# Reordering TensorE's slot in a Mamba-2 scan: square sums behind the off-diagonal products, group products ahead of the diagonal ones

## The chip, the cores and the metric

The kernel runs on one core of one Trainium2 chip (trn2). The metric is the device time of one execution in microseconds. Three runs of the kernel before gave 1118.15, 1118.6 and 1119.61 us; their median, 1118.6 us, is the time before.

## What is computed

The reference is two transformer-like blocks with adaptive layer norm. The first one holds the part that is changed: a Mamba-2 layer (32 heads of 128 channels, 8 groups, state size 128) over 2 batches of 512 tokens, model width 256. The rest (two mixture-of-experts layers and an attention layer over sorted keys) is the same in both kernels. Cut to the scan:

```python
hbc = silu(conv4(proj))                      # causal convolution of 4 taps, then hs, B, C
Y_diag = einsum('bclhn,bcshn,bhcls,bcshd->bclhd', Cc, Bc, Lmat, Xc)
states = einsum('bclhn,bhcl,bclhd->bchdn', Bc, decay_states, Xc)
Y_off  = einsum('bclhn,bchdn,bhcl->bclhd', Cc, states_prev, state_decay)
y = (Y_diag + Y_off).reshape(b, s, H, P) + D_res
g = (y * silu(gate)).reshape(b, s, I // gs, gs)      # gs = 512 channels = 4 heads
h = g * rsqrt(mean(g * g) + EPS)
return norm_w * h @ out_proj_w.T
```

The mean of squares runs over the 4 heads of one norm group. The kernel multiplies the unnormalised heads by the output weights and scales the product by the group's root afterwards.

## The kernel before, in words

The scan works on 64 pairs of batch and head (N = 64), in chunks of 128 tokens. It is a software pipeline of slots, s = 0 to 69, written out by hand: every engine has its own `scan_slot(s)`, and only semaphores tie them together. In slot s head s begins (`h0`), head s-1 is in its second slot (`h1`), head s-2 in its third (`h2`), and one tile of 128 tokens of an earlier norm group is projected out (`e`). Every fourth slot, with s mod 4 = 2, begins a new norm group for `e` (`e[0] == 0`). The text below calls a slot by **its kind, s mod 4** (kind 0 to 3); four slots are a period.

**TensorE, in order** (lines 502 to 582):

- px: six bf16 products of 512 columns, the x projection (L513, recorded as L439 with tile wA and wAl);
- kind 2 only, sq: sums over the partitions of the squares (L521), which wait for GpSimd's last addition of squares (`sq_add`);
- t: four transposes of the convolved head (L532), which wait for VectorE's xT (L1401);
- o: off-diagonal products (L540), which wait for the states (L1370);
- w: one tile of the output projection (L552);
- d: diagonal products (L564), which wait for Mm (L1341), Xdt (ScalarE, L938), and VectorE's yv (L1381) of the head before, whose bank they overwrite;
- s: state products (L573), which wait for GpSimd's Xw (L1825);
- group_slot (L576; lines 480 to 500), in slots 0 to 47 only: a part of the products of group 4 + s//4. Kind 0 and 1: g, a projection half of six products (L439 with tile wbs), for B and for C; kind 2: k, four transposes of B (L453); kind 3: m, the C x B products (L459);
- pg: six products, the gate projection.

**VectorE, in order** (lines 1321 to 1414): Mm (L1341), gs (L1345), yv (L1381, waits for o), three taps of the convolution (L1354), three state steps (L1367 for the first, a copy out of PSUM that waits for s; L1370 for the others), xT (L1401), acc (L1412, takes the tile of w). Then its own group_slot: three taps of the group (L1273) in kind 0 and 1, with BT (L1281) ahead of them in kind 1, and CT (L1289) in kind 2. In kind 2 the twelve steps of the root, `root(0)` to `root(11)`, each of 4 elements a partition, are strewn between these: step 0 (L1424) reads sq's sums out of PSUM, the others (L1427, L1432, L1435, L1437, L1440) read and write SBUF alone. BT and CT too read SBUF alone; the taps, Mm, gs, yv, xT and acc read PSUM.

**GpSimd, in order** (lines 1813 to 1861): Xw (L1825, waits for Xdt), yb = yv * gs (L1835, waits for yv), wAl (L1842), CE (L1846), wB scaled (L1852), sqa += ysq (L1858, not where the head is the first of its norm group, which is kind 2), and in kind 3 the mask of CB (L1810), which the trace shows at the start of the next slot. All of them read SBUF. ScalarE evaluates the tanh and exp functions and turns PSUM into SBUF; SyncE loads weights ahead of their use.

Of the kernel before, what the change touches and what calls it, by code (L numbers as in the profile page):

```python
# [8 lines left out]
B, S, D = 2, 512, 256  # L9
T = B * S  # L10
P = 128
KT = D // P
NT = T // P
TB = S // P
# [15 lines left out]
N = B * H  # L30
# [13 lines left out]
def build_block(nc, io, stop=None):  # L44
# [4 lines left out]
    with ctx:  # L49
# [6 lines left out]
        bank = [ctx.enter_context(nc.psum_tensor(f"bank{n}", [P, 512], fp32)) for n in range(8)]  # L56
# [8 lines left out]
        ident, tri, ones = cst[:, 0:P], cst[:, P:2 * P], cst[:, 2 * P:3 * P]  # L65
# [61 lines left out]
        sqa = sb("sqa", [P, 2, S])  # L127
# [107 lines left out]
        q = {n: sem(n) for n in names}  # L235
# [130 lines left out]
        def _(pe):  # L366
# [48 lines left out]
            for t in range(NT):  # L415
                for kt in range(KT):
                    last = nc.tensor.matmul(bank[4][:, t * H:(t + 1) * H], hT[:, kt, t * P:(t + 1) * P],
                                            wdt[:, kt, :], start=kt == 0, stop=kt == KT - 1)
# [11 lines left out]
            for b in range(B):  # L430
                last = nc.tensor.transpose(bank[7][:, b * P:(b + 1) * P], csq[:, b * P:(b + 1) * P], ident)
# [48 lines left out]
            def group_slot(s):  # L480

                gq, r = FIRST + s // 4, s % 4
                if gq >= B * G:
                    return
                if r == 0:
                    pe.wait_ge(q["c_evac"], 2 * gq)
                    if s == 0:
                        pe.wait_ge(q["csr_done"], 1)
                    group_half(gq, 0, bank[7][:, :]).then_inc(q["c_proj"], 1)
                if r == 1:  # L490
                    pe.wait_ge(q["c_step"], 6 * gq + 3)
                    group_half(gq, 1, bank[7][:, :]).then_inc(q["c_proj"], 1)
                if r == 2:
                    pe.wait_ge(q["c_step"], 6 * gq + 6)
                    pe.wait_ge(q["c_bc"], 2 * gq + 1)
                    turn_keys(bank[7])
                if r == 3:
                    pe.wait_ge(q["c_evac"], 2 * gq + 1)
                    pe.wait_ge(q["c_bc"], 2 * gq + 2)
                    meet(gq, bank[7])  # L500

            def scan_slot(s):

                h0, h1, h2, e = head(s), head(s - 1), head(s - 2), out_tile(s)
                if h0:
                    n, b, hid = h0
                    w = (wAh[:, n % 4, :], wAl[:, n % 2, :])
                    pe.wait_ge(q["wsplit"], n + 1)
                    if n == 0:
                        pe.wait_ge(q["c_step"], 6 * (FIRST - 1))  # L510
                    else:
                        pe.wait_ge(q["cv_step"], 3 * n)
                    split_product(bank[0][:, :], lambda a, kt: w[a][:, kt * P:(kt + 1) * P],  # L513
                                  lambda a, kt: hTs[:, a, kt, b * S:(b + 1) * S]).then_inc(q["px"], 1)
                if e and e[0] == 0:
                    k = e[1]
                    if s - 1 < N:
                        pe.wait_ge(q["rc_step"], 3 * (s - 1))
                    pe.wait_ge(q["sq_add"], 3 * (k + 1))
                    for t in range(TB):  # L520
                        last = nc.tensor.matmul(bank[4][:, S - P + t:S - P + t + 1], sqa[:, k % 2, t * P:(t + 1) * P],  # L521
                                                ones[:, 0:1], start=True, stop=True)
                    last.then_inc(q["ssq_done"], 1)
                if h1:
                    n = h1[0]
                    pe.wait_ge(q["xT_done"], n + 1)
                    if n:
                        pe.wait_ge(q["xdt_done"], n)
                    else:
                        pe.wait_ge(q["c_evac"], 2 * FIRST)  # L530
                    for t in range(TB):
                        last = nc.tensor.transpose(bank[2][:, t * P:(t + 1) * P],  # L532
                                                   xT[:, n % 4, t * P:(t + 1) * P], ident)
                    last.then_inc(q["tr_x"], 1)
                if h2:
                    n = h2[0]
                    pe.wait_ge(q["rc_step"], 3 * n + 3)
                    pe.wait_ge(q["ce_done"], n + 1)
                    for c in range(1, TB):
                        last = nc.tensor.matmul(bank[5][:, c * P:(c + 1) * P], St[:, n % 2, (c - 1) * P:c * P],  # L540
                                                CE[:, n % 2, (c - 1) * P:c * P], start=False, stop=True,
                                                skip_group_check=True)
                    last.then_inc(q["py"], 1)
                if e:
                    t, k = e
                    if t == 0:
                        pe.wait_ge(q["wo_done"], HG * (k + 1))
                        pe.wait_ge(q["yb_done"], HG * (k + 1))
                    if TB * k + t:
                        pe.wait_ge(q["oa_done"], TB * k + t)  # L550
                    for m in range(HG):
                        last = nc.tensor.matmul(bank[6][:, 0:D], yb[:, HG * (k % 2) + m, t * P:(t + 1) * P],  # L552
                                                wB[:, k % 2, m, :], start=m == 0, stop=m == HG - 1)
                    last.then_inc(q["out_done"], 1)
                if h1:
                    n = h1[0]
                    pe.wait_ge(q["xdt_done"], n + 1)
                    pe.wait_ge(q["M_done"], n + 1)
                    if n:
                        pe.wait_ge(q["yc_done"], n)  # L560
                    else:
                        pe.wait_ge(q["c_step"], 6 * FIRST)
                    for c in range(TB):
                        nc.tensor.matmul(bank[5][:, c * P:(c + 1) * P], Xdt[:, n % 2, c * P:(c + 1) * P],  # L564
                                         Mm[:, n % 2, c * P:(c + 1) * P], start=c == 0, stop=c == 0,
                                         skip_group_check=True)
                    if n:
                        pe.wait_ge(q["rc_step"], 3 * n)
                    if e and e[0] == 0:
                        pe.wait_ge(q["rg_step"], ROOT * e[1] + 1)  # L570
                    pe.wait_ge(q["xw_done"], n + 1)
                    for c in range(TB - 1):
                        last = nc.tensor.matmul(bank[4][:, c * P:(c + 1) * P], Btok[:, h1[2] % G, c, :],  # L573
                                                Xw[:, n % 2, c * P:(c + 1) * P], start=True, stop=True)
                    last.then_inc(q["ps"], 1)
                group_slot(s)  # L576
                if h0:
                    n, b, hid = h0
                    if n:
                        pe.wait_ge(q["gs_done"], n)  # L580
                    split_product(bank[1][:, :], lambda a, kt: w[a][:, (KT + kt) * P:(KT + kt + 1) * P],
                                  lambda a, kt: hTs[:, a, kt, b * S:(b + 1) * S]).then_inc(q["pg"], 1)
# [574 lines left out]
        def _(dve):  # L1157
# [147 lines left out]
            def group_slot(s):  # L1305

                gq, r = FIRST + s // 4, s % 4
                if gq >= B * G or r == 3:
                    return
                if r == 1:  # L1310
                    keys(gq)
                if r == 2:
                    queries(gq)
                    return
                dve.wait_ge(q["c_raw"], 2 * gq + r + 1)
                for d in (1, 2, 3):
                    if d > 1:
                        dve.wait_ge(q["c_step"], 6 * gq + 3 * r + d - 1)
                    group_tap(gq, r, d, bank[7])

            def scan_slot(s):
# [7 lines left out]
                def root(*steps):  # L1329

                    if e and e[0] == 0:
                        for k in steps:
                            root_step(k, e[1])

                if h1:
# [3 lines left out]
                    if n % H % (H // 2) < HG:  # L1339
# [4 lines left out]
                    dve.wait_ge(q["thg_done"], n + 1)  # L1344
                    nc.vector.scalar_tensor_tensor(out=gs[:, n % 4, :], in0=thg[:], scalar=1.0, in1=bank[1][:, :],  # L1345
                                                   op0=ALU.add, op1=ALU.mult).then_inc(q["gs_done"], 1)
                root(0)

                def tap(d):

# [21 lines left out]
                                                           in1=bank[4][:, c * P:(c + 1) * P],  # L1372
                                                           op0=ALU.mult, op1=ALU.add).then_inc(q["rc_step"], 1)

                root(1)
                if h2:
                    n, b, hid = h2
                    since("yb_done", n - 1)
# [2 lines left out]
                    nc.vector.scalar_tensor_tensor(out=yv[:, n % 2, :], in0=xT[:, n % 4, :],  # L1381
                                                   scalar=chn[:, hid, 5:6], in1=bank[5][:, :],
                                                   op0=ALU.mult, op1=ALU.add).then_inc(q["yc_done"], 1)
                root(2)
                tap(1)
                root(3)
                tap(2)
                root(4)
                tap(3)
# [14 lines left out]
                if e:  # L1404
                    t, k = e
# [586 lines left out]
```

## Time and profile before

| what | value |
|---|---|
| median of 3 runs | 1118.6 us (1118.15 to 1119.61) |
| the profiled execution's own time | 1124.9 us |
| its span, first to last instruction | 1122.9 us |
| TensorE busy | 914.9 us (81%) |
| VectorE busy | 891.4 us (79%) |
| ScalarE busy | 616.3 us (55%) |
| GpSimd busy | 515.3 us (46%) |
| mean granted TensorE clock | 0.906 |
| the scan, slots 1 to 63 | 88.7 to 618 us of the span |

Busy time is the sum of an engine's instructions; the span also holds its waits. In the timelines of the section below each row is one instruction, or several of one form in a row (x4): the start in us from the span's start, the duration, the engine, the line, the operation, what is written and read, and in brackets how long the engine was idle before it and who released it. Matmuls are pipelined, so a product that is recorded with 379 ns is followed by the next one 216 ns later; what a part costs is therefore read from its start to the start of what follows. An fp32 matmul has two records, so 4 transposes and 3 or 4 products of fp32 stand as x4, x6 and x8.

### The profile page before, as it was taken

The numbers are of one execution on the slowest core, as the hardware profiler recorded it, in microseconds if no ns is written. First come the engines' busy times: TensorE is split into PE (matmuls) and PEld (weight loads), VectorE is DVE, ScalarE is ACT, GpSimd is POOL, SyncE is SP. The second block draws the span as 40 slices with busy tenths as digits, with TensorE's granted clock in tenths as the row PEclk, the third lists the DMA queues.
The fourth block names the chain that finished last, engine by engine and source line by source line (L and its number), as shares of the span: only waits on it lengthen the run. The fifth ranks groups of instructions, "written<-read, shape, count | busy, mean of one in ns | idle before, by whom it ended". The sixth has DMA issues, their size and how long they took to land. (4 is left out here: it accounts for less than half of the span.)

```text
span 1122.9 us, 16807 instructions
## 1 busy us (share of the span) xinstructions
PE 914.9 (81%) x5377; PEld 614.3 (55%) x5454; DVE 891.4 (79%) x1663; ACT 616.3 (55%) x1312; POOL 515.3 (46%) x496
## 2 busy tenths in 40 slices
PE   5867899999999999999999658995169567836996
PEld 5635677767777767676767434453142252224554
DVE  5488999999999999998888496658989787567453
ACT  2247778777777777777777132222538526704111
POOL 0224766766776667777667243220800140007332
PEclk9689999999999999999999968996579767965999
DMA  6002321322222222213232030000100000012001
GB/s 244 33 10 75 95 75 58 84 86 76 75 73 79 76 76 89 81 57 95 76 94 58 0 138 1 1 1 29 28 1 1 0 2 0 1 52 81 1 1 38
DMA packets 33964, 60.14 MB, mean 54 GB/s; under 512 B 3490, under 2 KB 15778, under 8 KB 33058
## 3 DMA queue, kind: packets, MB, share of 16 engines
q1 hardware_dynamic: 33880, 59.10, 16.6%
q8 instruction: 44, 0.72, 0.3%
q14 instruction: 40, 0.33, 0.1%
HBM read 57.12 MB, written 1.18 MB: 52 GB/s over the span
## 5 line engine op out<-in xcount | busy, mean ns | idle before, releaser
L1354 DVE SCALAR_TENSOR_TENSOR u<-bank,chn,u 128x511 f32<-128x511 f32 (+2 forms) x192 | 142.8, 744 | 3.5
L1825 POOL TENSOR_TENSOR xbuf<-xbuf,dec 128x384 f32<-128x384 f32 x64 | 53.3, 833 | 160.2 <-ACT xbuf L938 135.4
L552 PE MATMUL bank<-wB,yb 128*128 128x256 f32 x512 | 124.4, 387 | 2.0 <-DVE acc L1412 2.0
L439 PE MATMUL bank<-hTs,wA 128*128 128x512 bf16 x456 | 120.3, 381 | 4.0 <-DVE u L1354 1.0
L552 PEld LDWEIGHTS bank<-wB,yb 128*128 128x128 f32 x512 | 94.0, 194 | 14.1 <-DVE acc L1412 3.5
L1885 POOL TENSOR_TENSOR hfl<-hf 128x512 bf16<-128x512 f32 x44 | 45.8, 1041 | 116.5 <-DVE hf L1536 62.9
L439 PE MATMUL bank<-hTs,w13s 128*128 128x512 bf16 x354 | 91.0, 405 | 7.6 <-DVE hTs L1209 3.1
L1835 POOL TENSOR_TENSOR yb<-yv,gs 128x512 f32<-128x512 f32 x64 | 81.8, 1277 | 8.9 <-DVE yv L1381 8.8
L1873 POOL TENSOR_TENSOR w13s<-w,w13s 128x256 bf16<-128x256 f32 (+1 forms) x22 | 23.9, 1118 | 134.2 <-ACT w13s L1001 134.1
L938 ACT ACTIVATE xbuf<-bank,dtv 128x128 f32<-128x128 f32 x256 | 72.9, 370 | 20.7 <-PE bank L532 20.5
L948 ACT ACTIVATE rel<-csb,cs 128x128 f32<-128x128 f32 x256 | 82.2, 413 | 0.0
L734 PE MATMUL bank<-Ex,VW 128*80 128x512 f32 x128 | 73.6, 665 | 10.5 <-ACT Ex L1115 9.5
L564 PE MATMUL bank<-Mm,xbuf 128*128 128x128 f32 x512 | 70.3, 281 | 13.4 <-DVE yv L1381 11.1
L439 PEld LDWEIGHTS bank<-hTs,wA 128*128 128x128 bf16 x512 | 50.1, 98 | 53.5 <-issue 3.5
L564 PEld LDWEIGHTS bank<-Mm,xbuf 128*128 128x128 f32 x512 | 65.9, 194 | 22.7 <-issue 14.2
L1107 ACT ACTIVATE aw<-bank,scl 128x512 f32<-128x512 f32 x64 | 43.4, 685 | 62.9 <-DVE scl L1695 49.6
L439 PE MATMUL bank<-hTs,wAl 128*128 128x512 bf16 x255 | 76.0, 379 | 0.2 <-issue 0.2
L930 ACT ACTIVATE u<-bank,chn 128x512 f32<-128x512 f32 x64 | 49.8, 778 | 36.7 <-PE bank L439 36.7
L1273 DVE SCALAR_TENSOR_TENSOR ug<-bank,bcp,ug 128x511 f32<-128x511 f32 (+2 forms) x84 | 61.9, 746 | 8.3 <-ACT ug L846 6.1
L1858 POOL TENSOR_TENSOR sqa<-sqa,ysq 128x512 f32<-128x512 f32 x48 | 66.9, 1394 | 0.6 <-ACT ysq L964 0.6
L1842 POOL TENSOR_TENSOR wAl<-wA 128x512 bf16<-128x512 f32 x63 | 66.6, 1057 | 0.0
L439 PEld LDWEIGHTS bank<-hTs,w13s 128*128 128x128 bf16 x372 | 38.1, 103 | 48.1 <-issue 9.4
(241 smaller groups left out, 2250.1 us busy)
## 6 DMA issues: line engine op xcount, KB each, us to landing
csb<-csd SPq DMA_DIRECT2D x64, 256.0 KB, 3.5
wA<-in_win SPq DMA_DIRECT2D x64, 256.0 KB, 3.8
wB<-in_wob SPq DMA_DIRECT2D x16, 512.0 KB, 5.5
w<-in_w SPq DMA_DIRECT2D x2, 1664.0 KB, 7.6
w<-in_w SPq DMA_DIRECT2D x1, 2304.0 KB, 9.1
CB<-in_wbc SPq DMA_DIRECT2D x1, 2048.0 KB, 13.6
yb<-in_wmod SPq DMA_DIRECT2D x1, 1536.0 KB, 9.1
Btok<-in_wmod SPq DMA_DIRECT2D x1, 1536.0 KB, 16.5
```

What stands on the lines that cost most here:

```text
L439: last = nc.tensor.matmul(out, wpart(a, kt), hpart(c, kt), start=n == 0, stop=n == 5)
L552: last = nc.tensor.matmul(bank[6][:, 0:D], yb[:, HG * (k % 2) + m, t * P:(t + 1) * P], wB[:, k % 2, m, :], start=m == 0, stop=m == HG - 1)
L564: nc.tensor.matmul(bank[5][:, c * P:(c + 1) * P], Xdt[:, n % 2, c * P:(c + 1) * P], Mm[:, n % 2, c * P:(c + 1) * P], start=c == 0, stop=c ...
L734: nc.tensor.matmul(bank[VB[par]][0:OC, :], VW[:, par, i * OC:(i + 1) * OC], Ex[:, i, :], start=i == 0, stop=i == 3).then_inc(q["a_PV"], 1)
L938: last = nc.scalar.activation(Xdt[:, n % 2, t * P:(t + 1) * P], bank[2][:, t * P:(t + 1) * P], ACT.Copy, scale=dtv[:, b * TB + t, hid:hid ...
L948: last = nc.scalar.activation(rel[:, t * P:(t + 1) * P], csb[:, n % 2, t * P:(t + 1) * P], ACT.Relu, scale=-1.0, bias=cs[:, b * TB + t, hi ...
L1273: nc.vector.scalar_tensor_tensor(out=o, in0=pa[:, 0:S - d], scalar=bcp[:, gq % G, m, 3 - d:4 - d], in1=o, op0=ALU.mult, op1=ALU.add).then_ ...
L1354: nc.vector.scalar_tensor_tensor(out=u[:, n % 2, d:S], in0=bank[0][:, 0:S - d], scalar=chn[:, hid, 3 - d:4 - d], in1=u[:, n % 2, d:S], op0 ...
L1825: nc.gpsimd.tensor_tensor(Xw[:, n % 2, :].rearrange("p (t n) -> p t n", n=P), Xdt[:, n % 2, 0:S - P].rearrange("p (t n) -> p t n", n=P), d ...
L1835: nc.gpsimd.tensor_tensor(yb[:, n % 8, :], yv[:, n % 2, :], gs[:, n % 4, :], ALU.mult)\
L1842: nc.gpsimd.tensor_tensor(wAl[:, (n + 1) % 2, :], wA[:, (n + 1) % 4, :], wAh[:, (n + 1) % 4, :], ALU.subtract).then_inc(q["wsplit"], 1)
L1858: nc.gpsimd.tensor_tensor(sqa[:, k % 2, :], sqa[:, k % 2, :], ysq[:], ALU.add)\
```

## The change

In TensorE's slot, sq moves from behind px to behind o, and group_slot from behind s to behind w, ahead of d. In VectorE's slot the steps of the root move: step 0 and 1 from ahead of yv to behind it, step 2 from ahead of the first tap to between the first and the second, where step 3 is; steps 4 to 11 stay. No instruction is added or dropped, and no wait.

```diff
@@ TensorE, scan_slot @@
                     split_product(bank[0][:, :], ...).then_inc(q["px"], 1)
-                if e and e[0] == 0:
-                    k = e[1]
-                    if s - 1 < N:
-                        pe.wait_ge(q["rc_step"], 3 * (s - 1))
-                    pe.wait_ge(q["sq_add"], 3 * (k + 1))
-                    for t in range(TB):
-                        last = nc.tensor.matmul(bank[4][:, S - P + t:S - P + t + 1], sqa[:, k % 2, t * P:(t + 1) * P],
-                                                ones[:, 0:1], start=True, stop=True)
-                    last.then_inc(q["ssq_done"], 1)
                 if h1:
...
                     last.then_inc(q["py"], 1)
+                if e and e[0] == 0:
+                    k = e[1]
+                    if s - 1 < N:
+                        pe.wait_ge(q["rc_step"], 3 * (s - 1))
+                    pe.wait_ge(q["sq_add"], 3 * (k + 1))
+                    for t in range(TB):
+                        last = nc.tensor.matmul(bank[4][:, S - P + t:S - P + t + 1], sqa[:, k % 2, t * P:(t + 1) * P],
+                                                ones[:, 0:1], start=True, stop=True)
+                    last.then_inc(q["ssq_done"], 1)
...
                     last.then_inc(q["out_done"], 1)
+                group_slot(s)
                 if h1:
...
                     last.then_inc(q["ps"], 1)
-                group_slot(s)
                 if h0:
@@ VectorE, scan_slot @@
-                root(0)
...
-                root(1)
                 if h2:
...
-                root(2)
+                root(0, 1)
                 tap(1)
-                root(3)
+                root(2, 3)
                 tap(2)
                 root(4)
                 tap(3)
```

## Rows read from the trace of the kernel before

**Rows 1.** Busy time per engine in one period, slots 32 to 35 (PE, PEld, DVE, ACT, POOL).
```profile
354.64:389.03 34.39, 33.23 (x206) 24.66 (x208) 32.12 (x65) 26.63 (x62) 23.89 (x26) 1.00 0.25 77
```

**Rows 2.** VectorE's waits over five periods, 217 to 389 us (total us, times, longest).
```profile
DVE yv L1381 <- PE bank L540: 5.2, 5, 1.0
```

**Rows 3.** Timeline of TensorE, slot 32 (kind 0) from t, into slot 33.
```profile
355.93 0.60 PE L532 MATMUL bank<-cst,xT 128*128 128x128 f32 x4
356.37 0.83 PE L540 MATMUL bank<-xbuf 128*128 128x128 f32 x6
357.04 1.89 PE L552 MATMUL bank<-wB,yb 128*128 128x256 f32 x8
358.77 1.05 PE L564 MATMUL bank<-Mm,xbuf 128*128 128x128 f32 x8
359.66 0.83 PE L573 MATMUL bank<-xbuf,Btok 128*128 128x128 f32 x6
360.33 1.46 PE L439 MATMUL bank<-hTs,wbs 128*128 128x512 bf16 x6
...
362.92 1.03 PE L439 MATMUL bank<-hTs,wA 128*128 128x512 bf16 x4
```

**Rows 4.** Timeline of VectorE, first state step of slot 32 and two rows of slot 33.
```profile
360.60 0.29 DVE L1367 COPY xbuf<-bank 128x128 f32<-128x128 f32 x1 [0.29 <-PE bank L573]
...
366.12 0.74 DVE L1381 SCALAR_TENSOR_TENSOR yv<-xT,chn,bank 128x512 f32<-128x512 f32 x1
...
370.97 0.68 DVE L1281 SCALAR_TENSOR_TENSOR BT<-thx,ug 128x512 f32<-128x512 f32 x1
```

**Rows 5.** Timeline of GpSimd, slots 33 (kind 1) and 34 (kind 2).
```profile
367.22 1.28 POOL L1835 TENSOR_TENSOR yb<-yv,gs 128x512 f32<-128x512 f32 x1
...
370.99 1.79 POOL L1858 TENSOR_TENSOR sqa<-sqa,ysq 128x512 f32<-128x512 f32 x1
...
376.64 1.28 POOL L1835 TENSOR_TENSOR yb<-yv,gs 128x512 f32<-128x512 f32 x1
```

**Rows 6.** Timeline, slot 5 (kind 1), where BT begins behind a GpSimd instruction.
```profile
129.74 0.61 POOL L1852 TENSOR_TENSOR wB<-wB,chn 128x256 f32<-128x256 f32 x1
129.90 1.01 DVE L1281 SCALAR_TENSOR_TENSOR BT<-thx,ug 128x512 f32<-128x512 f32 x1
```

**Rows 7.** Timeline of VectorE, slot 34 (kind 2), with root steps 0, 1 and 2.
```profile
374.98 0.16 DVE L1424 TENSOR_SCALAR ssv<-bank 128x4 f32<-128x4 f32 x1
375.18 0.17 DVE L1427 TENSOR_SCALAR nwt<-ssv 128x4 int32<-128x4 int32 x1
375.28 0.75 DVE L1381 SCALAR_TENSOR_TENSOR yv<-xT,chn,bank 128x512 f32<-128x512 f32 x1
375.95 0.76 DVE L1432 TENSOR_SCALAR rg<-nwt 128x4 int32<-128x4 int32 x1
...
378.86 0.73 DVE L1354 SCALAR_TENSOR_TENSOR u<-bank,chn,u 128x509 f32<-128x509 f32 x1
...
380.94 0.69 DVE L1401 SCALAR_TENSOR_TENSOR xT<-bank,u 128x512 f32<-128x512 f32 x1
```

**Rows 8.** Timeline of slot 35 (kind 3) and of o in slot 36.
```profile
381.68 0.66 PE L532 MATMUL bank<-cst,xT 128*128 128x128 f32 x4 [0.25 <-DVE xT L1401]
...
384.32 0.74 DVE L1381 SCALAR_TENSOR_TENSOR yv<-xT,chn,bank 128x512 f32<-128x512 f32 x1
...
385.20 1.13 PE L564 MATMUL bank<-Mm,xbuf 128*128 128x128 f32 x8 [0.47 <-DVE yv L1381]
385.23 1.28 POOL L1835 TENSOR_TENSOR yb<-yv,gs 128x512 f32<-128x512 f32 x1 [0.65 <-DVE yv L1381]
...
390.76 0.83 PE L540 MATMUL bank<-xbuf 128*128 128x128 f32 x6
```

**Rows 9.** Timeline of TensorE, sq in slot 58 (kind 2, no group products left).
```profile
571.86 1.02 PE L521 MATMUL bank<-cst,sqa 128*128 128x1 f32 x8 [1.03 <-POOL sqa L1858]
```

**Rows 10.** Waits in the first six slots, 84 to 131 us (total us, times, longest).
```profile
DVE yv L1381 <- PE bank L540: 1.9, 2, 1.1
```

## The prediction

> **What bounds the kernel now.** I read the busy time by period first. In a period of 34.39 us TensorE is busy for 33.23 and VectorE for 32.12 [rows 1]: both are nearly full, so neither view of busy time names the bound, and the order of the waits must. The ten periods of slots 8 to 47 repeat to 0.01 us (one of them has 0.37 more), so one period can be worked out and multiplied. Next I read the waits, then the timelines engine by engine. VectorE waits for o ahead of yv, 1.0 us once per period [rows 2], which is kind 0, and there 0.29 us for s ahead of its first state step [rows 4]. TensorE waits for xT ahead of t (0.25 us) and for yv ahead of d (0.47 us), both in kind 3 [rows 8]. This closes a loop, and the loop is the bound: o of kind 0 releases yv, but then s of the same slot releases VectorE's state step; from there VectorE runs without a wait through kind 1 to xT of kind 2; xT releases t of kind 3; from t TensorE runs, with the wait for yv, to o of the next kind 0. In rows: o 356.37, state 360.60 [rows 3, 4], xT 380.94 [rows 7], t 381.68, o 390.76 [rows 8]: 4.23 + 20.34 + 0.74 + 9.08 = 34.39 us. A part costs or gives time where it is on this loop, and nowhere else.
>
> **The change part by part.** The prices from start to start [rows 3]: t 0.44, o 0.67, w 1.73, d 0.89, s 0.67 us; g and pg together take 2.59, so 1.30 for six products of 512 columns, px too. k is 4 transposes, 0.44; m and sq are each 8 records of the form that d has, 0.89.
>
> 1. *g ahead of d in kind 0, 10 times (slots 8 to 44).* g now stands behind s, off the loop on the VectorE side. It moves into the leg from o to s: 4.23 becomes 5.53 us. VectorE already waits there, so nothing hides it: **+1.30**, and VectorE reaches everything in kind 1 1.30 us later. g needs only what ScalarE copied out a slot ago. In kind 1 g is covered: with yv at 367.42 to 368.16 (366.12 + 1.30, 0.74 long [rows 4]), d behind g would start at 365.32 + 1.73 + 1.30 = 368.35 (w of slot 33 is 8.95 us behind o of slot 32: two g or pg, px, t, o and the products between [rows 3]), and s ends 0.3 us ahead of VectorE's last tap: nothing.
> 2. *m ahead of d in kind 3, 11 times (slots 7 to 47).* d now waits for yv. The leg from xT to the next o holds the same instructions, only the wait goes: 0.74 + 0.49 (t after a wait, the 0.49 between its start and o's here) + 0.67 + 1.73 + m 0.89 + d 0.89 + s 0.67 + pg 1.29 + px 1.29 + t 0.44 = 9.10, against 9.82 now (390.76 - 380.94): **-0.72**.
> 3. *sq behind o, k ahead of d, in kind 2.* In the periods with groups TensorE has room in kind 2, where VectorE is the loop: the wait for the squares and the order cost or give nothing. t moves 1.1 us ahead; what hides all this is that room, and without it sq's 0.89 us would stand on the loop wherever it is put. In the four periods without groups sq waits 1.03 us [rows 9] and holds up t, o, yv. Behind o it starts at the same time, when the squares are there, and yv comes 2.1 us earlier (o right behind px and t). The first tap then comes 1.9 us earlier (step 1 meets Xw), the third 0.9, since steps 2 to 4 wait for GpSimd as in part 5, xT 1.1; in kind 3 d then waits for yv and takes back half: **-0.6**, 4 times. Bounds: 0 and -1.03 - 0.25.
> 4. *BT against GpSimd, kind 1, 10 times.* Where a VectorE instruction that reads only SBUF meets a running GpSimd instruction, one waits: BT took 1.01 us in place of 0.68, and ended 0.56 us behind wB's end (129.74 + 0.61) [rows 6]; with BT first, by 0.02 us, it took 0.68 and sqa 1.79 [rows 4, 5], against 1.28 for yb of the same size. Now the starts after the change: BT moves by 1.30, to 372.27. GpSimd's row is tied to yv: yb starts 0.17 us behind yv's end (384.32 + 0.74, 385.23 [rows 8]), so in slot 33 at 368.33, and sqa 3.77 us later, at 372.10. **GpSimd is now ahead, by 0.17 us.** BT waits until 372.10 + 1.28 = 373.38 and ends 0.56 later, 373.94, against 372.95 unblocked: **+0.99** on the loop. Bounds: 0, if BT still is first, and 1.28, a whole sqa.
> 5. *The root steps, kind 2, 11 times.* Step 2 took 0.76 us for 4 elements, where step 1 took 0.17 [rows 7]: it ended as GpSimd's Xw did and yb began (376.64 [rows 5]). Let Y be yv's start. Now steps 0 and 1 take 0.30 ahead of yv, and the third tap starts at Y + 3.58: 3.88 in all. After: step 0 at Y + 0.67, step 1 at Y + 0.87; yb wants to start at Y + 0.91, so step 1 is ahead by 0.04; tap 1 at Y + 0.97, step 2 at Y + 1.64, held until yb ends at Y + 2.32; step 3 meets the next GpSimd instruction (wAl, 1.04) and is held until Y + 3.32; tap 2, then step 4, held until CE ends, Y + 4.28; tap 3 at Y + 4.20. That is +0.32; steps 5 to 8 behind it then meet an idle GpSimd, -0.1: **+0.2**. If step 1 loses by those 0.04 us, it waits for all of yb, and the same count gives +1.0. I take +0.2, because in rows 4 and 5 a lead of 0.02 was enough.
> 6. *The first slots.* In slots 3 and 4 yv waits 1.9 us for an o that comes late behind a waiting d [rows 10]; k and m fill that wait: **-1.5**. Bounds 0 and -1.9.
>
> What a page says stands by itself here. The Trainium skill, page "SBUF — State Buffer", section "Who interferes with whom", says that a VectorE instruction with two SBUF inputs and a GpSimd instruction that reads SBUF exclude each other, and that whichever starts first holds the port for its whole length while the other fully blocks. The trace agrees in both directions (1.01 and 1.79 us above), and by this rule a lead of 0.17 us is enough for part 4. Were ports no matter, parts 4 and 5 would be nil and the sum +1.2.
>
> **Sum:** 10 x 1.30 - 11 x 0.72 - 4 x 0.6 + 10 x 0.99 + 11 x 0.2 - 1.5 = +13.3 us. A full period becomes 34.39 + 1.30 - 0.72 + 0.99 + 0.2 = 36.2 us. Against the profiled execution's 1124.9 us (span 1122.9) this is 1138; that execution is 6.3 us above the median, and nothing behind the scan changes, so I forecast the same difference on the median: 1118.6 + 13.3 = **1131.9 us**.
>
> **Rivals.**
> *A: BT stays first* (sqa is held up by something that I don't see, or a start on record is not yet a hold on the port). Then part 4 is nil: +3.4, 1122. For it: the margin is 0.17 us. Against: sqa follows yv by a chain of GpSimd instructions with no wait between them.
> *B: step 1 loses to yb,* by 0.04 us of my reckoning: +0.8 x 11 on top, +22, 1141.
> *C: no port matters,* the late BT and the root steps find GpSimd idle in places that I have put wrongly: +1.2, 1120, no change that can be measured (a measurement of this kernel tells some 0.2%, 2.2 us, from none).
> *D: faster. TensorE is the bound in fact.* The point that decides is the first state step of kind 0: if VectorE comes to it 1.3 us later than now, g ahead of s costs nothing. Then each of the 11 periods loses TensorE's 1.65 us of gaps (34.39 less the prices above: four slots of 6.98, and 4.82 for g, g, k, sq and m, 32.74), which with parts 3 and 6 is -22, 1097. For it: TensorE has 97% of the period, and d, sq and t do wait. Against: VectorE waits 0.29 us for s at that very place and about 1 us for o just ahead [rows 4, 2]. A half way case, where VectorE's delay takes away only its own slack, would give -5.
> *E: the change does nothing,* because all waits are set by something else: against it stands the loop, which closes to 0.01 us.
>
> **How the numbers follow.** Forecast 0.43, A 0.20, B 0.11, C 0.10, D with its half way case 0.15, E 0.01. Faster than by 0.2%: D, and a little of C, 0.17. Within 0.2%: the rest of C, E and a third of A, where a size a little off suffices: 0.16. Slower: 0.67. The range takes in A, C, B and the forecast with its bounds: 1116 to 1142; D is left out below. The forecast's own range is 1126 to 1137.
>
> **What would show it.** In the profile after: periods of 36.2 us in place of 34.39; VectorE's wait for s in kind 0 at about 1.6 us in place of 0.29, ten times; d of kind 3 without a wait; BT at 1.6 to 1.7 us in kind 1 and sqa at 1.28 (part 4), or BT 0.68 and sqa 1.79 (A); t of kind 3 waiting for xT 2 us or more; step 1 at 0.17 us (B: over 1 us); steps 2 and 3 at 0.7 to 1.0 us; the last four periods at 30.5 in place of 31.1 us. The forecast is wrong if VectorE's wait for s stays under 0.5 us, since then g is covered, or if the periods are below 34.4 us.

## The result, and the profile after

The changed kernel is slower. Over 22 runs of each its median is 1126.68 us against 1121.09 us, 5.6 us more; the means differ by 7.0 us, ratio 1.0062 (95% interval 1.0042 to 1.0083, which is +4.7 to +9.3 us). I had forecast slower, by 13.3 us, and a median of 1131.9 us, with 1126 to 1137 as the forecast's own range: 1126.68 lies at its lower edge. It lies inside partly by luck, because the three runs that the forecast started from had a median 2.5 us below that of the 22; from 1121.09 the same sum gives 1134.4. Its profiled execution took 1130.7 us with a span of 1128.7, against 1124.9 and 1122.9.

The span alone misleads, because TensorE's clock rose at another moment in the setup (granted clock from 80 to 84 us: 0.68 before, 0.96 after): o of slot 2 starts at 98.90 us before and at 94.33 after. So I count from that row to the addition of the scan's result to the residual, and cut the way at o of three slots (behind the addition, where both kernels are the same, the profile after is 3.0 us longer):

| stretch, us | before | after | difference |
|---|---|---|---|
| o of slot 2 to o of slot 8 | 51.13 | 48.74 | -2.39 |
| slots 8 to 48, ten periods with group products | 344.26 | 358.90 | +14.64 |
| slots 48 to 64, four periods without | 124.51 | 119.37 | -5.14 |
| o of slot 64 to the addition | 26.08 | 26.32 | +0.24 |
| sum | 545.98 | 553.33 | +7.35 |

The change costs 1.46 us in each of ten periods and gives back half of it at the two ends. Some 2.2 us of what comes back belong to the clock of the one execution profiled before, and not to the change. Some 1.5 us of them stand in the first stretch, where TensorE ran at the lower of its two clock levels in slot 2 (granted clock 0.50 from 102 to 105 us, 1.00 after), behind a wait of 2.32 us. Its d took 2.04 us there, in place of 1.13 in slot 3:

```profile
102.05 2.04 PE L564 MATMUL bank<-Mm,xbuf 128*128 128x128 f32 x8 [2.32 <-DVE yv L1381]
```

The other 0.7 us stand in slot 54 (point 3 below). A period now, in the view of busy time per stretch (PE, PEld, DVE, ACT, POOL; it answers to [rows 1]):

```profile
356.41:392.26 35.85, 33.17 (x205) 24.80 (x208) 32.94 (x66) 26.24 (x63) 23.42 (x25) 1.00 0.22 73
```

VectorE's 32.94 us of busy time are 0.82 more than in [rows 1], for the same work: some of its instructions now contain a wait. The waits of five periods of the kernel after, 213 to 392 us (total us, times, longest), the lines that bear on the loop; they answer to [rows 2]:

```profile
DVE xbuf L1366 <- PE bank L574: 7.9, 5, 1.6
...
PE bank L565 <- DVE yv L1379: 5.9, 5, 1.2
...
DVE yv L1379 <- PE bank L531: 2.4, 5, 0.5
...
PE bank L523 <- DVE xT L1399: 1.6, 5, 0.3
```

The first line is the state step of kind 0 (L1366 after is L1367 before): it waits 1.58 us for s in place of 0.29. The wait of yv for o, in kind 0 too, has halved. d's 1.2 us have moved to kind 2, where they stand beside the loop. The timeline of TensorE in a slot of kind 0, the answer to [rows 3], shows g between w and d:

```profile
358.14 0.83 PE L531 MATMUL bank<-xbuf 128*128 128x128 f32 x6
358.81 1.89 PE L552 MATMUL bank<-wB,yb 128*128 128x256 f32 x8
360.54 1.46 PE L439 MATMUL bank<-hTs,wbs 128*128 128x512 bf16 x6
361.84 1.05 PE L565 MATMUL bank<-Mm,xbuf 128*128 128x128 f32 x8
362.73 0.83 PE L574 MATMUL bank<-xbuf,Btok 128*128 128x128 f32 x6
```

The timeline of VectorE and GpSimd through the same period, the answer to [rows 4], [rows 5] and [rows 7] (L1366 first state step, L1856 sqa, L1281 BT, L1379 yv, L1425 root step 1, L1833 yb, L1430, L1433 and L1435 steps 2, 3 and 4, L1840 wAl, L1399 xT of kind 2):

```profile
363.67 0.29 DVE L1366 COPY xbuf<-bank 128x128 f32<-128x128 f32 x1 [1.58 <-PE bank L574]
...
373.72 1.27 POOL L1856 TENSOR_TENSOR sqa<-sqa,ysq 128x512 f32<-128x512 f32 x1
...
373.98 1.57 DVE L1281 SCALAR_TENSOR_TENSOR BT<-thx,ug 128x512 f32<-128x512 f32 x1
...
378.88 0.74 DVE L1379 SCALAR_TENSOR_TENSOR yv<-xT,chn,bank 128x512 f32<-128x512 f32 x1
...
379.73 0.17 DVE L1425 TENSOR_SCALAR nwt<-ssv 128x4 int32<-128x4 int32 x1
...
379.79 1.27 POOL L1833 TENSOR_TENSOR yb<-yv,gs 128x512 f32<-128x512 f32 x1 [2.48 <-DVE yv L1379]
380.47 0.62 DVE L1430 TENSOR_SCALAR rg<-nwt 128x4 int32<-128x4 int32 x1
...
381.01 1.05 POOL L1840 TENSOR_TENSOR wAl<-wA 128x512 bf16<-128x512 f32 x1
381.12 0.95 DVE L1433 TENSOR_TENSOR nwt<-rg 128x4 f32<-128x4 f32 x1
...
382.66 0.38 DVE L1435 SCALAR_TENSOR_TENSOR nwt<-nwt,ssv 128x4 f32<-128x4 f32 x1
...
384.87 0.69 DVE L1399 SCALAR_TENSOR_TENSOR xT<-bank,u 128x512 f32<-128x512 f32 x1
```

BT now starts 0.26 us behind sqa and takes 1.57 us; sqa is back at 1.27. Over the whole trace BT's median is 1.62 us, against 0.68 before. And the end of the loop, TensorE in kind 3, the answer to [rows 8]: t waits for xT, d does not wait.

```profile
385.62 0.66 PE L523 MATMUL bank<-cst,xT 128*128 128x128 f32 x4 [0.32 <-DVE xT L1399]
386.11 0.83 PE L531 MATMUL bank<-xbuf 128*128 128x128 f32 x6
386.78 1.89 PE L552 MATMUL bank<-wB,yb 128*128 128x256 f32 x8
388.51 1.05 PE L459 MATMUL bank<-CT,BT 128*128 128x128 f32 x8
389.40 1.06 PE L565 MATMUL bank<-Mm,xbuf 128*128 128x128 f32 x8
...
393.99 0.83 PE L531 MATMUL bank<-xbuf 128*128 128x128 f32 x6
```

The loop, leg by leg: o to the state step 358.14 to 363.67, 5.53 (was 4.23); state step to xT of kind 2, 363.67 to 384.87, 21.20 (was 20.34); xT to t 0.75 (was 0.74); t to the next o 8.37 (was 9.08). The sum is 35.85, the period. The changes are +1.30, +0.86, +0.01 and -0.71.

### The profile page after: what moved, and what is told of

Its sections match the earlier page's. It is cut to its first block and busy times, and to the rows that moved or that the text cites. A ratio compares the mean times of both kernels' runs of the same rounds, so it can differ in the third digit from the quotient of the medians.

```text
span 1128.7 us, 16807 instructions
## 1 busy us (share of the span) xinstructions
PE 910.7 (81%) x5377; PEld 612.5 (54%) x5454; DVE 899.8 (80%) x1663; ACT 610.9 (54%) x1312; POOL 509.4 (45%) x496
## 5 line engine op out<-in xcount | busy, mean ns | idle before, releaser
L1833 POOL TENSOR_TENSOR yb<-yv,gs 128x512 f32<-128x512 f32 x64 | 81.6, 1274 | 45.9 <-DVE yv L1379 45.4
L640 PE MATMUL bank<-w2s,hf 128*128 128x256 bf16 x352 | 63.3, 282 | 3.7 <-POOL hfl L1883 3.7
L1840 POOL TENSOR_TENSOR wAl<-wA 128x512 bf16<-128x512 f32 x63 | 65.6, 1041 | 0.0
```

The source lines that it names most:

```text
L640: last = nc.tensor.matmul(bank[6 + t // 2][:, (t % 2) * D:(t % 2 + 1) * D], (hfh, hfl)[a][:, m % 3, t * P:(t + 1) * P], w2s[:, c, f, :], s ...
L1833: nc.gpsimd.tensor_tensor(yb[:, n % 8, :], yv[:, n % 2, :], gs[:, n % 4, :], ALU.mult)\
L1840: nc.gpsimd.tensor_tensor(wAl[:, (n + 1) % 2, :], wA[:, (n + 1) % 4, :], wAh[:, (n + 1) % 4, :], ALU.subtract).then_inc(q["wsplit"], 1)
```

## The experiments

Theory 1 is the forecast's: the loop, with g of kind 0 and BT's wait for sqa on it. Its first rival was that sq and the root steps cost the time and the group products are neutral. In each diff below the minus lines are the changed kernel's, unless it says otherwise. Each ran beside the kernel before on the same chip. "Period" is that of slots 8 to 47, and "four last" the periods without group products.

**e1: g of kind 0 behind s again.**

```diff
-                group_slot(s)
+                if s % 4:
+                    group_slot(s)
...
                     last.then_inc(q["ps"], 1)
+                if s % 4 == 0:
+                    group_slot(s)
```

> The changed kernel with one thing undone: the group product of kind 0 (g) stands behind s again; g of kind 1, k and m stay ahead of d. Theory 1 (the loop o of kind 0, s of kind 0, xT of kind 2, t of kind 3, o): VectorE's wait for s in kind 0 goes back from 1.58 to 0.3 us, BT starts ahead of sqa again, and the period is 34.39 less the 0.71 of m, 33.7 us; the whole is 12 to 15 us faster than before (ratio 0.987 to 0.990). Theory 1 with BT still behind sqa: period 34.6, ratio about 0.996. Theory 2 (what costs time is sq and the root steps behind yv, the place of the group products is neutral): the period stays at 35.8 us, ratio 1.006.

Measured: ratio 1.0017 (1.0003 to 1.0030), period 34.90 us. Both theories miss. VectorE's state steps (L1369 here) in kind 0 and then kind 1:

```profile
355.55 0.29 DVE L1369 COPY xbuf<-bank 128x128 f32<-128x128 f32 x1 [0.28 <-PE bank L575]
...
365.13 0.29 DVE L1369 COPY xbuf<-bank 128x128 f32<-128x128 f32 x1 [1.08 <-PE bank L575]
...
367.15 0.68 DVE L1284 SCALAR_TENSOR_TENSOR BT<-thx,ug 128x512 f32<-128x512 f32 x1
```

The wait for s is gone from kind 0 and BT is back at 0.68, as theory 1 says. But a wait of 1.08 us has come up in kind 1: its g was hidden in the changed kernel only because VectorE came there 1.3 us late from kind 0. Without that delay g of kind 1 is on the loop itself. I had not asked what is next when a delay is taken away. Theory 1 mended: one g is paid per period, in the first of kinds 0 and 1 where VectorE is on time.

**e2: BT one place earlier on VectorE.**

```diff
-                if r == 1:
-                    keys(gq)
...
+                if s % 4 == 1 and FIRST + s // 4 < B * G:
+                    keys(FIRST + s // 4)
                 if e:
```

> The changed kernel with BT of kind 1 one place earlier in VectorE's order, ahead of acc, so that it starts 0.39 us earlier and 0.2 ahead of sqa. Theory 1 (BT waits for GpSimd's sqa, and that wait is on the loop): BT takes 0.68 in place of 1.62 us, sqa 1.7 to 1.9 in place of 1.28, the period falls from 35.85 to 34.95 us, ratio to before about 0.998. Rival (the wait only changes sides: a longer sqa now holds up sq, or BT's time is covered): the period stays at 35.85, ratio 1.006.

Measured: ratio 0.9998 (0.9981 to 1.0015), period 35.00 us: theory 1, the rival's 35.85 is out. The two rows of the race, in kind 1:

```profile
374.27 0.73 DVE L1281 SCALAR_TENSOR_TENSOR BT<-thx,ug 128x512 f32<-128x512 f32 x1
...
374.42 1.72 POOL L1856 TENSOR_TENSOR sqa<-sqa,ysq 128x512 f32<-128x512 f32 x1
```

With a lead of 0.15 us BT takes 0.73 and it is sqa that takes longer. The same instructions are issued and only two on VectorE change places: the 0.85 us per period are the port's. That a longer sqa now ends later costs nothing: sq, which needs it, starts 0.2 us late, in kind 2, beside the loop.

**e3: sq and the root steps alone** (the group products behind s, as before).

```diff
-                group_slot(s)
...
                     last.then_inc(q["ps"], 1)
+                group_slot(s)
```

> The kernel before with sq behind o and the root steps behind yv, the group products where they were, behind s. Theory 1: in the periods with group products nothing changes (34.39 us, at most 0.1 more), in the last four periods 31.07 becomes 29.95 us; 4 to 5 us faster in all, ratio 0.996. Theory 2 (this part is what costs): periods of 35 us and more, ratio over 1.004.

Measured: ratio 0.9961 (0.9943 to 0.9978), -4.4 us; period 34.44, the last full one 29.97 us against 31.08. Theory 1 holds, and the first rival falls: this half of the change is a gain, and in the trace all of it lies where no group products are left (124.51 to 119.41 us, of which 0.7 are the clock's).

**e4: the group products alone** (against the kernel before).

```diff
                     last.then_inc(q["out_done"], 1)
+                group_slot(s)
...
                     last.then_inc(q["ps"], 1)
-                group_slot(s)
```

> The kernel before with the group products ahead of d, sq and the root steps where they were. Theory 1: period 34.39 + 1.30 - 0.71 + 0.89 = 35.9 us if BT is held by sqa as in the changed kernel; sq then waits for nothing or little more; last four periods 31.07 as before; 10 to 13 us slower than before, ratio 1.009 to 1.012. Theory 2: period 34.4 us, ratio 0.997 to 1.000.

Measured: ratio 1.0100 (1.0073 to 1.0126), +11.2 us. The wait for s is 1.58 us and BT is held:

```profile
377.49 1.26 POOL L1858 TENSOR_TENSOR sqa<-sqa,ysq 128x512 f32<-128x512 f32 x1
...
377.74 1.55 DVE L1281 SCALAR_TENSOR_TENSOR BT<-thx,ug 128x512 f32<-128x512 f32 x1
```

The size came out, but not for the reasons given: the period is 35.34 us and not 35.9, and the first slots, which give 2 us back in the forecast, gave nothing in this trace (o of slot 2 to o of slot 8 takes 51.18 us against 51.13; both traces have stretches of lowered clock there). The stretch from gs to xT in kind 2 takes 6.10 us here, against 6.55 before, 6.59 after and 6.60 in e3. VectorE comes late to kind 2, so Xw is over before root step 2 begins, and step 2, directly behind yv, is still ahead of yb. It takes 0.16 us in place of the 0.76 of [rows 7]:

```profile
381.81 0.83 POOL L1825 TENSOR_TENSOR xbuf<-xbuf,dec 128x384 f32<-128x384 f32 x1 [3.07 <-ACT xbuf L938]
...
383.59 0.16 DVE L1432 TENSOR_SCALAR rg<-nwt 128x4 int32<-128x4 int32 x1
...
383.85 1.27 POOL L1835 TENSOR_TENSOR yb<-yv,gs 128x512 f32<-128x512 f32 x1 [1.20 <-DVE yv L1381]
```

In the changed kernel Xw is over in time too, but step 2 stands behind a tap and meets yb (0.62 us). So the root steps cost nothing against the kernel before (e3), but some 0.5 us per period against where they were, once the group products have moved. No run moved them without sq; the 0.49 us of the stretch on VectorE, which does not wait for sq there, are the evidence that it is the steps.

**e5: only k and m ahead of d**, g of kind 0 and 1 behind s.

```diff
-                group_slot(s)
+                if s % 4 > 1:
+                    group_slot(s)
...
                     last.then_inc(q["ps"], 1)
+                if s % 4 < 2:
+                    group_slot(s)
```

> The changed kernel with g of kind 0 and of kind 1 behind s again; only k (kind 2) and m (kind 3) stay ahead of d, sq and the root steps as changed. Theory 1, mended by the run with only kind 0 undone (a g ahead of d is paid once per period, in whichever of kind 0 and 1 VectorE comes to it without a delay): VectorE's wait for s is 0.3 us in kind 0 and nil in kind 1, d of kind 3 does not wait, the period is 34.44 - 0.71 = 33.7 us, and the whole is 13 to 16 us faster than before (ratio 0.986 to 0.989). Rival (m ahead of d frees nothing, the loop closes elsewhere): period 34.3 to 34.5, ratio 0.996.

Measured: ratio 0.9883 (0.9854 to 0.9912), -13.1 us, period 33.73 us. Theory 1 mended, to 0.03 us (one of the ten periods in the trace took 34.87); this is a version that beats both kernels. Its period in the view of busy time, and VectorE's waits of five periods, 213 to 382 us:

```profile
340.39:374.12 33.73, 32.97 (x205) 24.72 (x209) 32.12 (x66) 26.42 (x63) 23.91 (x24) 1.00 0.24 79
```

```profile
DVE yv L1382 <- PE bank L531: 2.4, 5, 0.5
DVE xbuf L1369 <- PE bank L575: 1.4, 5, 0.3
```

VectorE's busy time is back at the 32.12 us of [rows 1], which is the port's share seen from the other side, and the wait for s is 0.3 us, once per period.

**e6: g of kind 1 alone behind s.** The edit is that of e1 with `s % 4 != 1` and `s % 4 == 1`.

> The changed kernel with g of kind 1 alone behind s again. Theory 1, mended: in the changed kernel g of kind 1 is hidden, because VectorE comes to its state step 1.3 us late from kind 0; so nothing is gained: VectorE's wait for s in kind 0 stays 1.58 us, BT stays behind sqa (about 1.6 us), the period stays at 35.8 to 35.9 us, ratio 1.006. Rival (each g ahead of d costs its share): the period falls to 34.9 to 35.3 us, ratio 0.998 to 1.001.

Measured: ratio 1.0076 (1.0054 to 1.0097), period 35.85 us, the changed kernel's to 0.01. Rows of kinds 0 and 1 (L566 is d, L1369 the state step, L1284 BT):

```profile
363.31 0.29 DVE L1369 COPY xbuf<-bank 128x128 f32<-128x128 f32 x1 [1.58 <-PE bank L575]
...
369.57 1.13 PE L566 MATMUL bank<-Mm,xbuf 128*128 128x128 f32 x8 [0.95 <-DVE yv L1382]
...
373.53 1.65 DVE L1284 SCALAR_TENSOR_TENSOR BT<-thx,ug 128x512 f32<-128x512 f32 x1
```

With g out of kind 1, d waits 0.95 us for yv there: g had only filled that wait. e1, e5 and e6 together settle that the price is per period and not per product: both g ahead 35.85, g of kind 0 alone 35.85, g of kind 1 alone 34.90, none 33.73.

**e7: e5, with root steps 1 to 11 behind xT.**

```diff
-                root(0, 1)
+                root(0)
                 tap(1)
-                root(2, 3)
                 tap(2)
-                root(4)
                 tap(3)
                 state(0)
-                root(5)
                 state(1)
-                root(6)
                 state(2)
-                root(7, 8)
...
-                root(9, 10, 11)
+                root(*range(1, 12))
```

> The kernel with only k and m ahead of d, and root steps 1 to 11 all behind xT in kind 2, where GpSimd is idle; step 0 stays behind yv. Theory (the small SBUF-only steps cost what they wait for GpSimd's running instructions): each step takes 0.15 to 0.17 us, none 0.4 or more, the stretch from yv to xT in kind 2 is 1.4 to 1.7 us shorter, t of kind 3 starts earlier by that, then d of kind 3 waits about 1 us for yv; period 33.2 to 33.5 us, ratio about 0.985. Rival (the steps cost their issue wherever they stand, VectorE is only rearranged): period 33.7 us as without the move, ratio 0.987 to 0.989.

Measured: ratio 0.9897 (0.9874 to 0.9920), period 33.75 us. The steps take 0.16 to 0.17 us each, as expected, and xT leaves the loop: t of kind 3 waits for nothing. But acc of kind 2 needs the root, and w of kind 3 needs acc's PSUM bank. Root steps 10 and 11, acc, and w of kind 3:

```profile
369.97 0.16 DVE L1433 SCALAR_TENSOR_TENSOR nwt<-nwt,ssv 128x4 f32<-128x4 f32 x1
370.17 0.16 DVE L1436 SCALAR_TENSOR_TENSOR rg<-nwt,rg 128x4 f32<-128x4 f32 x1
370.37 0.48 DVE L1408 SCALAR_TENSOR_TENSOR acc<-bank,rg,acc 128x256 f32<-128x256 f32 x1
...
370.91 1.99 PE L552 MATMUL bank<-wB,yb 128*128 128x256 f32 x8 [0.69 <-DVE acc L1408]
```

A new wait of 0.69 us takes the place of what was freed, and VectorE's first state step of kind 2 now waits 0.51 us for s (none in the changed kernel). The period is the rival's, but its reason (the steps cost their issue wherever they stand) is not what the rows show. A second bank for w, which would tell how much is behind that wait, was not tried, so what closes the period here is argued and not shown.

## Why the prediction was right, and where it was not

The direction held, and so did the loop, g and m on it, and BT's wait for sqa. The sum was 6 us above the 7.35 of the table: the root steps were sized too large and the gain at the end too small. With the clock's 2.2 us left out of the table the change costs some 9.5 us in the scan, so 3.8 us of the 6 are the forecast's own error and the rest is the clock of one execution. Point by point:

1. *g in kind 0.* Forecast +1.30 per period and a wait of about 1.6 us for s; measured +1.30 and 1.58. That g of kind 1 is covered held too (e6), but I wrote it down as a property of kind 1, where it is a consequence of kind 0: e1 showed it.
2. *m in kind 3.* Forecast -0.72, measured -0.71; d waits no more. e5, which adds only k and m ahead of d to what e3 has, confirms it: 34.44 (e3) to 33.73.
3. *sq in the four periods without groups.* Forecast -0.6 each, measured 29.95 against 31.08, -1.1. The failed step is "in kind 3 d then waits for yv and takes back half". xT did come 1.1 us earlier as worked out, but the recorded text gives no number for the wait behind it; I had taken the 3.38 us from xT to yv from a period with group products, CT (0.60) included. Without groups there is no CT: in the kernel after, xT 583.51 to yv 586.29 is 2.78 us, and d, at 587.18, hardly waits. This term is -4.5 in place of -2.4, and the trace of before also had a stretch of lowered clock in slot 54 (granted clock 0.83 from 540 to 550 us, 0.7 us longer than its neighbours), which makes the table's -5.14.
4. *BT against GpSimd.* Forecast: GpSimd ahead by 0.17 us, BT held, +0.99. Measured: ahead by 0.20 in most periods (0.26 in the rows above), BT 1.62 us, and the stretch from BT to the next tap is 1.54 to 1.56 us in most periods in place of 0.60, +0.95 (1.49 in the rows above). What the forecast lacked is a small gain on the same leg in kind 0: VectorE's first tap of the group starts 0.39 us behind acc in place of 0.52, because ScalarE's copy of g's products is over by then (before, the copy ended at 362.67 and the tap began at 362.70). e2 turned the race round and took 0.85 us off the period. Rival A is out.
5. *The root steps.* Forecast +0.2, with step 1 ahead of yb by 0.04 us; measured ahead by 0.06 us in ten of the 11 periods (by more in slot 6) and 0.17 us long in all of them, so rival B is out; steps 2, 3 and 4 take 0.62, 0.95 and 0.38 us, held as counted. The term itself is nearly 0: gs to xT 6.59 us in place of 6.55. I let tap 3 start at Y + 4.20; it starts at 382.96, Y + 4.08.
6. *The first slots.* Forecast -1.5, with -0.7 for m in slot 7 and +0.2 for the steps in slot 6, -2.0; measured -2.4 up to o of slot 8, but this agreement is luck. The trace of e2 also has the lower clock in slot 2 (0.53 from 102 to 105 us) and from o of slot 3 to o of slot 8 its slots take what those of the changed kernel take, to 0.02 us. From o of slot 2 to o of slot 3 it takes 10.03 us against 8.52. So with the clock that the kernel before had, the first stretch would be some 50.25 us, and the change is worth about -0.9 there: -1.5 was too large.

One sign of the forecast missed: t of kind 3 was to wait 2 us or more for xT, and waits 0.32. TensorE's slack in kind 2 is taken up earlier, by d's wait for yv (1.17 us) and by pg's for VectorE's last tap (0.98).

The forecast period was 36.16, the measured one 35.85 us: 0.31 us too many in ten periods, 3 us of the 6; the other 3 are in points 3 and 6 (2.7 and 0.4). Without the clock's share they are 2.1 and -1.1, so the two ends erred in opposite directions. Rivals C and D are out with the loop's legs: no leg got shorter but the last, and VectorE did wait for s. C falls with BT's 1.62 us too.

The Trainium skill, page "SBUF — State Buffer", section "Who interferes with whom", has whoever starts first holding the shared port for the whole instruction. The trace agrees in both orders that the runs made: with BT ahead by 0.15 us it is sqa that takes 1.72 us (e2), with BT behind by 0.2 us it is BT that takes 1.62 (after). Step 1, ahead of yb by 0.06 us, says less: it is not held (0.17 us), but yb's 1.27 us show no wait either.

## What to carry to other kernels

When two engines are both over 90% busy, look for the loop of waits that closes over a period, sum its legs until they make the period, and price each move by the leg that it lands on: the same six products cost 1.3 us in one slot, nothing in the next, and 1.2 there once the first is mended. Filler work belongs ahead of an instruction that waits (m ahead of d in kind 3) and not ahead of one that others wait for (s in kind 0). And before a stretch of a trace is booked to a change, compare its granted clock in both traces: 2.2 us of 7.5 were the clock's here. An order that rests on a lead of 0.02 us at a shared port is not to be relied on: any delay on one side flips it.

## What the hardware showed that I had not expected

A held instruction does not lose the whole of the other's time: BT, 0.68 us alone, started 0.26 us into a sqa of 1.27 us and took 1.57, so it ended 0.56 us behind sqa's end, as it did behind wB's in [rows 6]. That is 0.1 us less than its own 0.68 (by the recorded starts and ends). And an instruction of 4 elements a partition, 0.16 us alone, is held as fully as a large one: root step 3 took 0.95 us behind wAl, until wAl ended, where the eleven steps of e7, with GpSimd idle, took 1.8 us of busy time together. So a chain of tiny steps strewn among large ones costs up to one GpSimd instruction per step.
